# Row maxima of head pairs: the causal mask added by VectorE inside its maximum, an instruction a head on diagonal tiles

## The reference, cut to what matters

```python
# B = 4 sequences of S = 1024 rows
q = (x @ wq.T).reshape(B, S, 16, 8)          # 16 query heads of 8
k = (x @ wk.T).reshape(B, S, 4, 8)           # 4 key heads, each shared by 4 query heads
attn = einsum('bqhd,bkhd->bhqk', q, k) / sqrt(8)
attn = where(tril(ones(S, S)), attn, -inf)   # causal mask
attn = softmax(attn, axis=-1)                # needs each row's maximum over the allowed keys
out = einsum('bhqk,bkhd->bqhd', attn, v) @ wo.T
```

## Time and profile before

| what | value |
|---|---|
| median of 3 runs | 1531.12 us |
| the profiled execution's own time | 1534.44 us |
| its span | 1533.2 us |
| PE busy | 1190.1 us (78%) |
| DVE busy | 1087.2 us (71%) |
| ACT busy | 731.0 us (48%) |
| POOL busy | 703.3 us (46%) |
| mask matmuls, line 611 | 512, 76.9 us busy, mean 235 ns |
| maxima, line 1176 | 384, 350.0 us busy, mean 949 ns |
| granted clock of PE over the run | 0.889 of full speed |

### The profile page before, as it was taken

One profiled execution on the slowest core, in us unless ns is written; L12 is line 12 of the kernel. 1 busy time (PEld: TensorE's weight loads), 2 busy tenths in 40 slices (PEclk: granted clock), 3 DMA queues, 4 the chain that ended last, 5 costly groups with the idle time before them and its releaser, 6 DMA issues.

```text
span 1533.2 us, 19558 instructions
## 1 busy us (share of the span) xinstructions
PE 1190.1 (78%) x6080; PEld 531.2 (35%) x6080; DVE 1087.2 (71%) x2107; ACT 731.0 (48%) x1599; POOL 703.3 (46%) x857
## 2 busy tenths in 40 slices
PE   3414896999998885567656788998999899989863
PEld 1212454555444443234222322333333333333221
DVE  5898645758988898678977575586878677776022
ACT  4634683255344343132310466556565656565741
POOL 7433673457777777447640131133413341334244
PEclk9755998999999988777875798899999999999996
DMA  3000104321111100011250413221032305010010
GB/s 105 0 1 0 47 1 111 85 73 60 42 48 35 35 15 0 0 23 45 50 83 26 70 27 54 56 44 41 13 71 35 50 10 75 18 25 4 1 42 14
DMA packets 42790, 58.75 MB, mean 38 GB/s; under 512 B 8080, under 2 KB 21136, under 8 KB 42400
## 3 DMA queue, kind: packets, MB, share of 16 engines
q1 hardware_dynamic: 40096, 55.60, 17.0%
q10 hardware_dynamic: 2592, 1.90, 0.4%
HBM read 50.79 MB, written 6.68 MB: 37 GB/s over the span
## 4 chain that ended last, share of the span: by engine, by line
PE 32%; DVE 18%; ACT 6%; issue 5%; POOL 3%; DMA 1%; SPq 1%; ACTq 0%; DVEq 0%; POOLq 0%
PE PS L683 8%; PE PS L666 6%; DVE SS L1176 6%; PE PS L606 5%; PE PS L728 3%; DVE RB L1113 2%; ACT RB L1596 2%; PE PS L611 2%; PE PS L319 2%; PE PS L510 2%; DVE st L768 2%; DMA B<-scrQ 1%; DVE B L1113 1%; ACT RB L1603 1%; DVE PS L1093 1%
## 5 line engine op out<-in xcount | busy, mean ns | idle before, releaser
L1596 ACT ACTIVATE RB<-PS 128x512 f32<-128x512 f32 (+3 forms) x768 | 324.0, 494 | 226.1 <-PE PS L666 224.4
L1176 DVE TENSOR_REDUCE SS<-PS 128x2 f32<-128x1024 f32 (+3 forms) x384 | 350.0, 949 | 73.5 <-PE PS L611 36.9
L1845 POOL TENSOR_SCALAR_AFFINE_SELECT RB<-RB 128x512 f32<-128x512 f32 x128 | 81.2, 635 | 407.8 <-ACT RB L1596 407.8
L666 PE MATMUL PS<-B 96*128 96x512 bf16 (+3 forms) x768 | 200.2, 338 | 17.6 <-ACT RB L1596 16.5
L683 PE MATMUL PS<-RB,B 128*32 128x512 f32 (+3 forms) x1536 | 171.0, 518 | 15.0 <-ACT RB L1603 15.0
L606 PE MATMUL PS<-B 64*128 64x512 bf16 (+3 forms) x768 | 136.4, 354 | 59.3 <-DVE SS L1176 29.3
L1764 POOL TENSOR_TENSOR RB<-RB,B 128x512 f32<-128x512 f32 x64 | 82.4, 1290 | 87.3 <-DVE RB L1006 66.1
L606 PEld LDWEIGHTS PS<-B 64*128 64x128 bf16 x768 | 39.0, 94 | 213.7 <-DVE SS L1176 88.9
L510 PE MATMUL PS<-B,WW 128*128 128x512 f32 x128 | 78.5, 746 | 38.6 <-DVE RB L1113 28.4
L1441 ACT ACTIVATE RB<-PS 128x512 f32<-128x512 f32 x72 | 42.8, 596 | 127.1 <-PE PS L422 127.0
L437 PEld LDWEIGHTS PS<-B,RB 128*128 128x128 f32 x576 | 77.4, 197 | 42.2 <-issue 27.9
(11 more groups left out here) (243 smaller groups left out, 2234.4 us busy)
## 6 DMA issues: line engine op xcount, KB each, us to landing
B<-scrQ SPq DMA_DIRECT2D x272, 64.0 KB
B<-scrW SPq DMA_DIRECT2D x128, 128.0 KB, 3.1
B<-scrK SPq DMA_DIRECT2D x200, 32.0 KB
scrQ<-B SPq DMA_DIRECT2D x6, 384.0 KB, 2.6
X<-in_x SPq DMA_DIRECT2D x8, 256.0 KB, 9.6
out_dram<-X SPq DMA_DIRECT2D x8, 256.0 KB, 3.0
B<-in_w SPq DMA_DIRECT2D x3, 576.0 KB, 4.9
B<-in_rope SPq DMA_DIRECT2D x1, 1024.0 KB, 12.2
```

The costliest lines, as they stand in the source:

```text
L666: pe.matmul(p[:, 0:w], KS[u % 2][:, kl, 128 * kt:128 * kt + 128], QS[u % 2][kl][:, z, 512 * qc + off:512 * qc + 512], start=True, stop=Tru ...
L1176: dve.tensor_reduce(MX[:, u % 2, i, 2 * h:2 * h + 2, c], p, AX, ALU.max).then_inc(s["mx1"], 1)
L1596: act.activation(RB[:, 4 * (step % 3) + z, 0:w], bank(bank_of["score", step, z])[:, 0:w], ACT.Exp).then_inc(s["ex2"], 1)
L1845: pool.affine_select(out=pb, in_=pb, compare_op=ALU.is_ge, fill=0.0, base=0, pattern=[[0, 4], [1, 128]], channel_multiplier=-1).then_inc(s ...
```

## The change: what it does

On the diagonal PE no longer runs the two mask matmuls; the pair's score matmuls end the pair. DVE there runs, in the place of one `tensor_reduce` over both heads, one `tensor_tensor_reduce` for each head: it reads the head's scores from PSUM and the mask from SBUF, adds them, writes the sum back to the same place in PSUM, and writes the maximum to `MX`. The mask tile is 512 columns wide (384 of zeros ahead of the 128x128 triangle), and a piece of width w uses its last w columns. Off the diagonal (128 pairs) nothing changes but the counting: `mx1` is now raised by two for a pair, so that on the diagonal a bank comes free head by head.

```diff
-        identb, msk = sb("w_identb", [128, 128], BF), sb("w_msk", [128, 128], BF)
+        identb, msk = sb("w_identb", [128, 128], BF), sb("w_msk", [128, 512], BF)
...
+        LOWEST = -3.0e38
...
                     ins = pe.matmul(bank(k + z)[:, 0:w], QM[u % 2][64 * z:64 * z + 64, h, 128 * i:128 * i + 128],
                                     KM[u % 2][64 * z:64 * z + 64, h // 2, 512 * c:512 * c + w],
-                                    start=True, stop=(c < i // 4), skip_group_check=True)
-                if c == i // 4:
-                    for z in range(2):
-                        ins = pe.matmul(bank(k + z)[:, w - 128:w], identb[:, :], msk[:, :], start=False, stop=True,
-                                        skip_group_check=True)
+                                    start=True, stop=True, skip_group_check=True)
                 ins.then_inc(s["mm1"], 1)
                 for z in range(2):
-                    banks.lend(k + z, s["mx1"], 48 * u + n + 1)
+                    banks.lend(k + z, s["mx1"], 96 * u + 2 * n + (z + 1 if c == i // 4 else 2))
...
-                p = bank(bank_of["first", u, n], 2).rearrange("p (z t) -> p z t", z=2)[:, :, 0:first_width(i, c)]
-                dve.tensor_reduce(MX[:, u % 2, i, 2 * h:2 * h + 2, c], p, AX, ALU.max).then_inc(s["mx1"], 1)
+                k, w = bank_of["first", u, n], first_width(i, c)
+                if c == i // 4:
+                    for z in range(2):
+                        p = bank(k + z)[:, 0:w]
+                        dve.tensor_tensor_reduce(p, p, msk[:, 512 - w:512], 1.0, LOWEST, ALU.add, ALU.max,
+                                                 MX[:, u % 2, i, 2 * h + z, c:c + 1]).then_inc(s["mx1"], 1)
+                else:
+                    p = bank(k, 2).rearrange("p (z t) -> p z t", z=2)
+                    dve.tensor_reduce(MX[:, u % 2, i, 2 * h:2 * h + 2, c], p, AX, ALU.max).then_inc(s["mx1"], 2)
...
-                dve.wait_ge(s["mx1"], 48 * u + 48)
+                dve.wait_ge(s["mx1"], 96 * u + 96)
...
-    D["msk"] = np.where(low, 0, -1e30).astype(bf)
+    D["msk"] = np.concatenate([np.zeros((128, 384)), np.where(low, 0, -1e30)], axis=1).astype(bf)
```

## The result

The changed kernel took 1543.5 us, the median of 17 runs (1536.2 to 1559.0), against 1535.6 us for the kernel before in 17 runs (1530.2 to 1545.9). The ratio is 1.0058 with a 95% interval of 1.0032 to 1.0085, so it is 5 to 13 us slower. The forecast was 7 us faster. The time lies inside the range, 1508 to 1545, but on the other side of no change.

What follows compares the result with a forecast made beforehand. PE was taken as the main limit and DVE as the second, handing over through a ring of two places. PE's -20.0 us and DVE's +12.7 us gave -7.3 us, from 1531.1 to 1524 us; range 1508 to 1545.

Steps and rivals of the forecast that it cites:

- The price on DVE: On each of 256 diagonal pairs DVE takes +0.20 us more, 51 us in all, of which 12.7 us count.
- 63.7: Microseconds added to the span per us added to a diagonal pair on DVE, by the maxima's shares of the chain.
- dear maximum: Rival: the maximum waits for the stream's end, DVE becomes the limit; at +0.50 us a pair 1552 us; chance 0.22.
- I keep 60% of 33.4: a gain of 20.0 us (2.7, 5.8 and 11.6 by stretch): Mask matmuls' chain charge in the first pass, stretches 779 to 845, 845 to 1000, 1000 to 1410 us: 60% is saved.
- half-worked lower end: Low end of PE's gain: half of 20.0 us, if PE's time comes back as a wait for ACT or DVE.
- covered: Rival: PE's time comes back as waits for the exponential and the ring, 10 us kept; about 1534 us; chance 0.10.
- The last 123 us keep their times: The end of the span, which holds no first-pass pair, was to take as long as before.
- PE's waits for DVE longer than 33.5 and 34.4 us: Sign: first-pass weight loads wait longer for DVE than the 33.5 us of the last stretch and 34.4 of the first.
- Unit 0's stretch longer by 1 us: Sign: from unit 0's first pair to its last, about 1 us longer.
- The long stretch shorter by 4 to 8 us: Sign: 1000 to 1410 us, where PE is 92% busy, shortens by only 4 to 8 us.
- A granted clock below 1.00 after 1000 us: Named as a sign that the prediction is wrong; PE's clock was full from 1000 to 1410 us.
- The rival of the clock: Fewer matmuls lower the clock of the middle stretch from 0.85 to 0.75, costing 12 us: 1536 us; chance 0.04.

Runs made afterwards that it cites:

- e1: Kernel before with the first pass's mask matmuls taken out and nothing put in, DVE's maxima as before: 1527.6 us, ratio 0.9941; again 1529.0 us, 0.9955.
- e2: Changed kernel with PE's mask matmuls kept as well, so the mask is added on both engines: 1551.9 us, ratio 1.0111 to the kernel before.
- e4: Kernel before, mask matmuls kept, with DVE's maxima cut to the first 128 columns of each head: 1508.1 us, ratio 0.9821.
- e5: Kernel before without the mask matmuls, and DVE's maxima cut to the first 128 columns of each head: 1493.7 us, ratio 0.9728.
- e9: Kernel before, mask matmuls kept, with DVE's maxima and ACT's exponentials both cut to the first 128 columns: 1480.9 us, ratio 0.9636.
- e10: Kernel before without the mask matmuls, DVE's maxima and ACT's exponentials both cut to the first 128 columns: 1458.6 us, ratio 0.9493.
- e11: Changed kernel with only the mask addition on each diagonal head, the maxima left out: 1529.7 us, ratio 0.9963 to the kernel before.
- e3: Changed kernel with a plain maximum for each diagonal head, no mask on either engine: 1537.3 us, ratio 1.0011 to the kernel before.

## Why the prediction was wrong, by its steps

**The price on DVE was right, its effect somewhat low.** +0.20 us a pair was charged, +0.175 measured. By the shares of the chain that is 63.7 x 0.175 = 11.1 us in the three stretches. From the mean of e1's two traces to the mean of the changed kernel's two it is 3.9 + 5.6 + 6.4 = 15.9 us. From before to e2's one trace it is 12.5, and e2's ratio gives 17 us, of which some 6 fall in the last stretch by that trace. In the even units the share from the chain (18.5%) was nearly what arrived (22%). Of the rivals, *dear maximum* is refuted: it needed 0.31 us a pair. The Trainium skill's statement of two instructions (VectorE: DVE Perf Modes, "Two Vector instructions with no wait between them") agrees with this trace, 512 accumulator reads beside 512 operations. The figure of about 75 ns an instruction that the prediction quoted from the Trainium skill (Vector Engine (DVE) Microarchitecture Reference, "Measured stream behaviour on trn2") was too high here, 58 measured.

**The step that failed: "I keep 60% of 33.4: a gain of 20.0 us (2.7, 5.8 and 11.6 by stretch)".** e1 gives it by itself: 2.0, 5.4 and 3.9, in all 11.3, and the last stretch takes half of that back. The first two are near the prediction, the second in part by luck of the clock in unit 2; the long stretch gives a third of its 11.6: 1.2 us in each of two even units and 0.5 in each of three odd ones at like clock. Its 163 pairs hold 19.6 us of mask matmuls at 0.12 us, so a fifth of that time came back, not 60% of the chain's charge. My half-worked lower end (half of 20.0, time handed back as waits) and the rival *covered* were the right idea, with its chance of 0.10 far too low.

**Where PE's time went in the long stretch.** A line's share of the chain says what the end hung on in this execution. It doesn't say how long the next chain is. The chains of waits of one even unit show it. Before:

```profile
by line: PE PS L683 23.7%; PE PS L666 18.4%; PE PS L606 14.2%; PE PS L611 6.3%; issue 6.2%; DVE SS L1176 5.2%; PE PS L319 4.9%; ACT RB L1596 4.4%; ACT RB L1603 3.4%; DVE st L768 2.4%; PE PS L708 1.7%; ACT RB L1324 1.5%; DVE XA L1247 1.0%; P
```

e1, the mask matmuls gone and DVE's work the same:

```profile
by line: PE PS L679 22.4%; PE PS L662 20.4%; PE PS L606 13.4%; DVE SS L1172 12.4%; issue 6.7%; PE PS L319 5.0%; ACT RB L1592 3.6%; ACT RB L1599 2.7%; DVE st L764 2.4%; PE PS L704 1.7%; ACT RB L1320 1.3%; DVE XA L1243 1.1%; PE PS L651 0.9%; 
```

The changed kernel:

```profile
by line: PE PS L682 18.7%; PE PS L665 16.1%; DVE PS L1178 13.3%; PE PS L609 10.4%; DVE SS L1182 9.1%; issue 7.5%; PE PS L322 5.2%; ACT RB L1602 3.6%; ACT RB L1609 2.6%; DVE st L767 2.3%; DVE SS L1178 1.8%; PE PS L707 1.7%; ACT RB L1330 1.2%
```

DVE's maxima are 5.2% of 66.2 = 3.4 us of it before, 12.4% of 65.0 = 8.1 us in e1 though they do the same work, and 24.2% (three groups) of 66.2 = 16.0 us after. Another chain, through DVE, lay close behind PE's. The experiments say that it isn't DVE's alone: of 3.8 us of mask matmuls an even unit gives back 1.2 with both engines full (before to e1), 1.6 with DVE light (e4 to e5) and 2.5 with DVE and ACT light (e9 to e10). The last 1.3 of 3.8 us did not come back even then; they went mostly into ten waits of one mask pair's time each, for ACT's copy and exponentials and for places of the ring. With both engines full the same is seen in before and e1 as longer waits of the score's weight loads for the exponential, 3.1 and 5.3 us in the unit (a wait of a weight load is not all lost, since it overlaps matmuls):

```profile
PEld PS L666 <- ACT RB L1596: 3.1, 13, 0.7
...
PEld PS L662 <- ACT RB L1592: 5.3, 21, 0.8
```

**The sum for an even unit**: -1.2 for PE, +1.2 for DVE, and 66.2 again. An odd unit: -0.5, +1.1, and 88.6 for 88.0. For the whole long stretch: predicted -11.6 + 6.0 = -5.6, measured -3.9 + 6.4 = +2.4 (means of two traces, 398.2 to 400.6); some 1.7 of it are the three odd units at like clock, and the rest goes with one more odd unit at clock 0.98 in each trace of the changed kernel. The stretches of unit 0 and of units 1 and 2 are 1.6 and 0.2 us longer in the means, the latter from 170.2 and 165.7.

**"The last 123 us keep their times" was wrong too.** Their work is the same, their clock isn't: 130.2 us at 0.79 in e1, 123.5 and 124.7 at 0.86 before, 124.6 and 126.3 at 0.86 and 0.84 in the changed kernel. For the change it is about +1.4 us; for e1 it takes 6 us of an 11 us gain. It isn't the number of matmuls ahead of it that decides: e2 keeps them all and has 130.3 us at 0.79, the changed kernel has 512 fewer and is at 0.84 and 0.86. What does is open.

**What the prediction asked the profile to show.** Two rows a head: yes. PE's waits for DVE longer than 33.5 and 34.4 us: yes, in the changed kernel's stretches from 1007 to 1419 and from 783.5 to 849 us:

```profile
PEld PS L609 <- DVE SS L1178: 46.9, 80, 1.7
...
PEld PS L609 <- DVE SS L1182: 11.3, 15, 1.2
...
PEld PS L609 <- DVE SS L1178: 26.6, 27, 4.4
PEld PS L609 <- DVE SS L1182: 20.0, 12, 3.9
```

That is 58.2 and 46.6 us. Unit 0's stretch longer by 1 us: 1.6. The long stretch shorter by 4 to 8 us: no, and that is the error. A granted clock below 1.00 after 1000 us, named as a sign of being wrong: yes, 0.99 over the long stretch in both traces, the extra dip above. The rival of the clock had the middle stretch at 0.75; it was 0.84. In unit 0's stretch, where no engine is full, the clock did fall, from 0.66 and 0.63 to 0.60 and 0.55.

**The faster version.** e1 beats both kernels: 0.9941 and 0.9955 of before, and some 1% below the changed kernel. It subtracts the maximum over future keys too, which a softmax cancels; how far such a maximum may lie above the causal one for other inputs was not tried.

## What to carry to other kernels

Where PE, DVE and ACT are busy for 92, 75 and 59% of a stretch and hand work to each other over two or three places, taking time from the first gives back only what the next chain lets through: a third of it in the even units here, an eighth in the odd ones. Moving work is then priced at both ends by one run each (take it out here, put it in there). Compare a stretch at the same granted clock: there the two runs added up to 0.1 us, while whole times moved by 5 us and more with the clock of stretches that the edit doesn't touch. An operation that yields a stream and a maximum is two starts a head on DVE, so one instruction over both heads that needs no mask costs DVE less than two that carry it.

## What the runs showed of the hardware

- The accumulator's read has a row of 142 ns of its own but adds only some 0.058 us before the next operation starts; in the trace it starts together with it. Heads of 512 columns start 0.65 us apart with the read and 0.60 apart in e11, which has none (two in 1.29 us, the last 0.69). Adding a mask from SBUF to scores in PSUM and writing them back costs DVE nothing per column: 689 ns against 680 at 512 columns and 288 against 280 at 128 (e11 and e3), and even units of 65.5 us with it and 65.4 without.
- With fewer matmuls in unit 0's stretch, where PE is busy for two thirds, the clock granted to TensorE is lower: 0.66 and 0.63 in the two traces of before and 0.58 in both traces of e1; e2, which has the mask matmuls again, is at 0.62. In the last stretch, whose matmuls are the same in all kernels, it is 0.86 (before, 124.7 and 123.5 us) and 0.79 (e1, 130.2 us in both traces; e2, 130.3; e3, 130.8). That follows the kernel, but not its mask matmuls, which e2 has and e1 and e3 have not.
